# Transposing the last four pairs of h0 by DMA in a graph layer on one NeuronCore

## The reference

```
h0  = relu(layernorm(x))
agg = adj @ h0                                  # the aggregate
h   = h0 @ W_sa ;  sl = h @ a_left ;  sr = h @ a_right
e   = where(adj != 0, exp(-leaky_relu(sl[:, None] + sr[None, :], 0.01)), 0)
x_a = (e @ h) / (sum(e, axis=1) + 1e-5)
x_b = agg @ W_gcnb + b_gcnb
attn_a = sigmoid([agg, h0] @ Wa.T + ba) ; attn_b the same with Wb, bb
out = x + sigmoid(attn_a * x_a + attn_b * x_b)
```

## Time and profile before

| | us |
|---|---|
| median of 3 runs | 179.05 (178.74 to 179.24) |
| profiled execution, its own time | 178.25 |
| its span | 176.4 |
| PE busy | 171.6 |
| DVE busy | 147.0 |
| ACT busy | 115.4 |
| POOL busy | 18.6 |

### The profile page before, as it was taken

How to read it: one execution, slowest core, us unless ns; L and a number is a source line. 1 busy time by engine, 2 the same in 40 slices (tenths; PEclk the granted TensorE clock), 3 DMA queues, 4 the chain that set the end, 5 groups by cost and what they waited for, 6 DMA issues and landing times.

```text
span 176.4 us, 3397 instructions
## 1 busy us (share of the span) xinstructions
PE 171.6 (97%) x1324; PEld 125.8 (71%) x1324; DVE 147.0 (83%) x309; ACT 115.4 (65%) x169; POOL 18.6 (11%) x42
## 2 busy tenths in 40 slices
PE   7999999999999999999999999999999999999992
PEld 2556776654444468888844488888888888888892
DVE  3799997648999999799999922999999999976551
ACT  3679899642899988748494640675875884863310
POOL 4745436030000200000000000000000000000000
PEclk9999999999999999999999999999999999999999
DMA  5999996999991598000001100000010010011101
GB/s 129 288 260 260 224 181 116 202 206 211 298 423 43 82 214 180 0 4 2 0 4 59 59 0 4 0 0 0 4 59 0 6 59 0 4 61 59 60 33 30
DMA packets 5520, 16.87 MB, mean 96 GB/s; under 512 B 625, under 2 KB 1409, under 8 KB 4737
## 3 DMA queue, kind: packets, MB, share of 16 engines
q0 software_dynamic: 1584, 8.39, 24.6%
q1 hardware_dynamic: 3920, 8.27, 13.2%
HBM read 22.94 MB, written 2.11 MB: 142 GB/s over the span
## 4 chain that ended last, share of the span: by engine, by line
PE 94%; DMA 3%; DVE 1%; SPq 1%; issue 0%; ACT 0%; DVEq 0%
PE ps L773 31%; PE ps L815 16%; PE ps L816 16%; PE ps L814 16%; PE ps L751 6%; PE ps L807 6%; DMA wa_sb<-in_w_wide 3%; PE ps L745 2%; SPq L234 1%; PE ps L877 0%; DVE wa_hi L507 0%; DVE logit L724 0%; DVE e_lo L526 0%; ACT logit L411 0%; DVE res L631 0%
## 5 line engine op out<-in xcount | busy, mean ns | idle before, releaser
L814 PE MATMUL ps<-mv_lo,e_hi 128*128 128x257 f16 (+2 forms) x272 | 71.0, 267 | 0.0
L816 PE MATMUL ps<-mv_hi,e_lo 128*128 128x257 f16 (+2 forms) x272 | 70.8, 266 | 0.0
L815 PE MATMUL ps<-mv_hi,e_hi 128*128 128x257 f16 (+2 forms) x272 | 70.8, 266 | 0.0
L377 ACT ACTIVATE z<-z,log_e 128x1024 f32<-128x1024 f32 x32 | 36.7, 1146 | 29.1 <-DVE z L568 29.1
L568 DVE SCALAR_TENSOR_TENSOR z<-sl_row,exs,far 128x512 f32<-128x512 f32 x64 | 45.0, 743 | 0.0
L576 DVE TENSOR_TENSOR e_lo<-z,e_hi 128x1024 f16<-128x1024 f32 x32 | 38.9, 1216 | 1.2 <-ACT e_hi L387 1.2
L773 PE MATMUL ps<-adj,nat_lo 128*128 128x512 f16 x128 | 36.8, 379 | 0.0
L773 PE MATMUL ps<-adj,nat_hi 128*128 128x512 f16 x128 | 36.7, 379 | 0.0
L387 ACT ACTIVATE e_hi<-z 128x1024 f16<-128x1024 f32 x32 | 33.3, 1041 | 0.0
L815 PEld LDWEIGHTS ps<-mv_hi,e_hi 128*128 128x128 f16 x272 | 26.5, 98 | 3.2
L814 PEld LDWEIGHTS ps<-mv_lo,e_hi 128*128 128x128 f16 x272 | 26.4, 97 | 3.3
(11 more groups left out here) (69 smaller groups left out, 164.8 us busy)
## 6 DMA issues: line engine op xcount, KB each, us to landing
adj<-in_adj_t POOLq DMA_DIRECT2D x6, 1024.0 KB, 10.4
x_sb<-in_x SPq DMA_DIRECT2D x6, 512.0 KB, 8.9
out<-res SPq DMA_DIRECT2D x7, 256.0 KB, 2.0
adj<-in_adj_t POOLq DMA_DIRECT2D x3, 512.0 KB, 7.5
x_sb<-in_x SPq DMA_DIRECT2D x3, 256.0 KB, 4.8
sl_row<-sl_line SPq DMA_DIRECT2D x1, 768.0 KB, 9.7
adj<-in_adj_t POOLq DMA_DIRECT2D x2, 256.0 KB, 5.9
wa_sb<-in_w_wide SPq DMA_DIRECT2D x1, 258.0 KB, 4.5
```

The lines of the kernel that those rows point to most:

```text
L377: act.activation(z[:, n % ZRING, :, :], z[:, n % ZRING, :, :], ACT.Exp, bias=log_e[:, 0:1], scale=SLOPE - 1.0).then_inc(exp_done, 1)
L814: pe.matmul(ps[:, bank, cols], e_hi[:, s, i1], mv_lo[:, j, cols], start=(j == 0), stop=False)
L815: pe.matmul(ps[:, bank, cols], e_hi[:, s, i1], mv_hi[:, j, cols], start=False, stop=False)
L816: return pe.matmul(ps[:, bank, cols], e_lo[:, s, i1], mv_hi[:, j, cols], start=False, stop=(j == NT - 1))
```

## The change

- Only units 0 to 4 (pairs 0 to 3) are still transposed by PE. For pairs 4 to 7, SP issues two transposing DMAs a pair, one from nat_hi into h0t_hi, one from nat_lo into h0t_lo, 128 partitions x 512 f16 each (turn_by_dma). ACT and DVE no longer copy these four pairs out of PSUM.
- The wide products of these four pairs leave the pair loop of chunk 0. They stand in the second aggregate, behind 8, 10, 13 and 16 of its 16 tiles. Their narrow_results, mv_highs and mv_lows move between the exponential steps n = 2 to 7.
- The sl row is made in two halves of 8 tiles. The first half is turned on PE behind pair 5 of chunk 0, and its store stands on SP behind the transposes of pairs 4, 5 and 6, its spread behind those of pair 7. The second store stands behind the reload of x.
- On POOL, load 5 is issued before norms(6) where it stood behind it, and loads 7 and 8 wait until all eight transposing DMAs have landed.
- h0t is laid out tile by tile. The adding of 0.5 to x (half_added) moves to steps 8, 9, 11 and 12.

```diff
-SL_PARTS = ((0, 4), (4, 16))
+SL_PARTS = ((0, 8), (8, 16))
+LATE = 4
+ONTIME = NPAIR - LATE
+NTURN = NU - LATE
-WIDE_BANKS = (6, 2)
+WIDE_BANKS = (6, 2, 6, 2, 0, 2, 0, 2)
@@ SP
+            def turn_by_dma(p):
+                ts = slice(2 * p, 2 * p + 2)
+                for have, nat, h0t in ((nat_high, nat_hi, h0t_hi), (nat_ready, nat_lo, h0t_lo)):
+                    sp.wait_ge(have, p + 1)
+                    sp.dma_start(h0t[:, ts, :, :].rearrange("p t k n -> p (t k) n"),
+                                 nat[:, ts, :].rearrange("p t d -> p (t d)"),
+                                 transpose=True).then_inc(h0t_landed[p - ONTIME], 16)
+
+            sp.wait_ge(adj_landed[piece_of(0, NT - 1)], 16)
+            turn_by_dma(4)
+            turn_by_dma(5)
+            turn_by_dma(6)
             sl_store(0)
+            turn_by_dma(7)
             sl_spread(0)
-            sl_store(1)
-            sp.wait_ge(turned, NU)
+            sp.wait_ge(adj_landed[piece_of(2, 0)], 16)
+            sp.wait_ge(turned, NTURN)
...
+            sl_store(1)
             sl_spread(1)
@@ POOL
             norms(5)
+            load_adj(5)
             norms(6)
-            load_adj(5)
             norms(7)
             norms(8)
             load_adj(6)
+            for p in range(ONTIME, NPAIR):
+                pool.wait_ge(h0t_landed[p - ONTIME], 32)
             load_adj(7)
             load_adj(8)
@@ ACT
-            for p in range(1, NPAIR):
...
+            for p in range(1, ONTIME):
+                if p + 2 < NTURN:
                     h0t_highs(p + 2)
+                h0_tiles(p + 3)
+                nat_highs(p + 2)
+                if p < ONTIME - 1:
+                    mv_highs(p)
+            h0_tiles(NU - 2)
+            nat_highs(NPAIR - 2)
+            mv_highs(ONTIME - 1)
+            h0_tiles(NU - 1)
+            nat_highs(NPAIR - 1)
+            sl_lines(0)
             agg_highs(0)
...
+                if n == 2:
+                    mv_highs(4)
+                if n == 3:
+                    mv_highs(5)
+                if n == 5:
+                    mv_highs(6)
                 if n == 6:
+                    mv_highs(7)
@@ DVE
+                if ONTIME <= n < NPAIR:
+                    dve.wait_ge(exs_ready, n + 1)
...
+                if n == 2:
+                    narrow_results(4)
+                if n == 3:
+                    mv_lows(4)
+                    narrow_results(5)
+                if n == 4:
+                    mv_lows(5)
+                if n == 5:
+                    narrow_results(6)
+                if n == 6:
+                    mv_lows(6)
+                    narrow_results(7)
                 if n == 7:
+                    mv_lows(7)
+                if n == 8:
                     agg_lows(1)
@@ PE
                 b_pair(p)
-                if p + 1 < NPAIR:
+                if p + 2 < NTURN:
                     turn(p + 2)
-                wide(p + 1)
-            b_products(1, 0, 4)
-            pe.wait_ge(h0t_ready, NU)
-            sl_lines(1)
-            b_products(1, 4, 16)
-            b_products(2, 0, 16)
+                if p + 1 < NTURN:
+                    wide(p + 1)
+                if p == 5:
+                    pe.wait_ge(mv_ready, 6)
+                    sl_lines(0)
+            b_products(1, 0, 8)
+            pe.wait_ge(h0t_ready, NTURN)
+            wide(5)
+            b_products(1, 8, 10)
+            wide(6)
+            b_products(1, 10, 13)
+            wide(7)
+            b_products(1, 13, 16)
+            wide(8)
+            b_products(2, 0, 4)
+            sl_lines(1)
+            b_products(2, 4, 16)
```

More of the change, by code:

```diff
@@ L53 @@
 NU = len(UNITS)
-SL_PARTS = ((0, 4), (4, 16))
-SL_UNIT = 4
-SL_BANKS = (2, 0)
+SL_PARTS = ((0, 8), (8, 16))
+SL_BANKS = (6, 0)
 SL_COLS = slice(BANK - P, BANK)
 X_PARTS = ((0, 1), (1, 2), (2, 4), (4, 6), (6, 8), (8, 12), (12, 16))
-WIDE_BANKS = (6, 2)
+LATE = 4
+ONTIME = NPAIR - LATE
+NTURN = NU - LATE
+WIDE_BANKS = (6, 2, 6, 2, 0, 2, 0, 2)
 B_BANKS = (4, 6, 4, 4)
@@ L119, in build @@
         e_lo = sb("e_lo", [P, 2 * ESLOT, CW], F16)
-        h0t_hi = e_hi[:, 16:24, :].rearrange("p (k s) n -> p k (s n)", k=KT)
-        h0t_lo = e_lo[:, 16:24, :].rearrange("p (k s) n -> p k (s n)", k=KT)
+        h0t_hi = e_hi[:, 16:24, :].rearrange("p s (a k n) -> p (s a) k n", k=KT, n=P)
+        h0t_lo = e_lo[:, 16:24, :].rearrange("p s (a k n) -> p (s a) k n", k=KT, n=P)
         zeros = e_hi[:, 0, :]
@@ L136, in build @@
         part_b = sb("part_b", [P, 2, D], F32)
-        sl_turn = [part_b[0:hi - lo, h, 0:P] for h, (lo, hi) in enumerate(SL_PARTS)]
+        sl_turn = [c_sb[0:hi - lo, C_WT + h * P:C_WT + (h + 1) * P] for h, (lo, hi) in enumerate(SL_PARTS)]
         gated_b = sb("gated_b", [P, 2, 2, D], F32)
@@ L172, in build @@
         h0t_ready = sem("h0t_ready")
+        h0t_landed = [sem(f"h0t_landed{p}") for p in range(ONTIME, NPAIR)]
         wide_product = sem("wide_product")
@@ L219, in turn_bank, with h0t_tiles @@
             n = (UNITS[u][1] - UNITS[u][0]) * P
-            return ps[:, u % 2, 0:KT * n].rearrange("p (k n) -> p k n", k=KT)
-        def h0t_cols(tile, u):
-            return tile[:, :, UNITS[u][0] * P:UNITS[u][1] * P]
+            return ps[:, u % 2, 0:KT * n].rearrange("p (t k n) -> p t k n", k=KT, n=P)
+        def h0t_tiles(tile, u):
+            return tile[:, UNITS[u][0]:UNITS[u][1], :, :]
         def wide_bank(t):
-            return WIDE_BANKS[t // 2 % 2] + t % 2
+            return WIDE_BANKS[t // 2] + t % 2
         block = ctx.enter_context(nc.Block())
@@ L344, in h0t_highs @@
                 act.wait_ge(turned, u + 1)
-                act.activation(h0t_cols(h0t_hi, u), turn_bank(u), ACT.Copy).then_inc(h0t_high, 1)
+                act.activation(h0t_tiles(h0t_hi, u), turn_bank(u), ACT.Copy).then_inc(h0t_high, 1)
             def nat_highs(p):
@@ L353, in mv_highs @@
                 act.wait_ge(exs_ready, p + 1)
-                if p == SL_UNIT - 1:
-                    sl_lines(0)
                 act.activation(scale_a[:, 2 * p:2 * p + 2], exs[:, 2 * p:2 * p + 2, SR], ACT.Exp, bias=log_s[:, 0:1],
@@ L442, in _ @@
                     act_high(n - 1)
-                if n in (2, 3, 4):
-                    half_added(n - 2)
+                if n == 2:
[4 more added lines that the diff above has]
+                    mv_highs(6)
                 if n == 6:
+                    mv_highs(7)
+                    act.activation(factor_l[:, :], exs[:, :, SL], ACT.Exp, scale=SLOPE).then_inc(factors_done, 1)
+                if n == 7:
                     agg_highs(1)
-                    half_added(3)
+                if n == 8:
+                    sl_lines(1)
+                if n in (8, 9, 11, 12):
+                    half_added((8, 9, 11, 12).index(n))
                 if n == 10:
@@ L525, in h0t_lows @@
                 dve.wait_ge(h0t_high, u + 1)
-                dve.tensor_tensor(h0t_cols(h0t_lo, u), turn_bank(u), h0t_cols(h0t_hi, u), ALU.subtract).then_inc(h0t_ready, 1)
+                dve.tensor_tensor(h0t_tiles(h0t_lo, u), turn_bank(u), h0t_tiles(h0t_hi, u), ALU.subtract).then_inc(h0t_ready, 1)
             def nat_lows(p):
@@ L562, in dve_z @@
                 if j == 0:
-                    dve.wait_ge(sl_ready[min(c, 1)], 16)
+                    dve.wait_ge(sl_ready[c // 2], 16)
                 if n >= ZRING:
@@ L651, in _ @@
             mv_lows(0)
-            for p in range(1, NPAIR):
-                if p + 1 < NPAIR:
-                    nat_lows(p + 1)
+            for p in range(1, ONTIME - 1):
+                nat_lows(p + 1)
                 if p > 1:
                     mv_lows(p - 1)
-                if p + 4 < NU:
-                    moments(p + 4)
+                moments(p + 4)
                 narrow_results(p)
-                if p + 1 < NPAIR:
-                    h0t_lows(p + 2)
-            mv_lows(NPAIR - 1)
+                h0t_lows(p + 2)
+            moments(NU - 2)
+            nat_lows(ONTIME)
+            mv_lows(ONTIME - 2)
+            moments(NU - 1)
+            narrow_results(ONTIME - 1)
+            for p in range(ONTIME + 1, NPAIR):
+                nat_lows(p)
+            mv_lows(ONTIME - 1)
             agg_lows(0)
@@ L743, in turn @@
                     for k in range(KT):
-                        cols = slice((t - UNITS[u][0]) * P, (t - UNITS[u][0] + 1) * P)
-                        ins = pe.transpose(turn_bank(u)[:, k, cols], x_sb[:, t, k * P:(k + 1) * P], ident[:, :])
+                        ins = pe.transpose(turn_bank(u)[:, t - UNITS[u][0], k, :], x_sb[:, t, k * P:(k + 1) * P], ident[:, :])
                 ins.then_inc(turned, 1)
@@ L750, in wide_part @@
                     for k in range(KT):
-                        ins = pe.matmul(ps[:, wide_bank(t), cols], h0t[a][:, k, t * P:(t + 1) * P], wa2[b][:, k, cols],
+                        ins = pe.matmul(ps[:, wide_bank(t), cols], h0t[a][:, t, k, :], wa2[b][:, k, cols],
```

(9 more changed lines are left out.)

## The result

The changed kernel takes 190.3 us (median of 6, 188.8 to 193.9) against 179.15 for the kernel before: a ratio of 1.062 (95% interval 1.056 to 1.067). It is slower by 11 us, in the predicted direction, inside the stated range of 177 to 192 and near its upper end; the forecast of 185.0 was 5.3 us too low. The loss is thus nearly twice the forecast one, 11 us where 6 were forecast.

What follows compares the result with a forecast made beforehand. PE work plus PE's waits was taken to bound the kernel: 178.25 less 1.76 for turns, plus 6.7 wait at wide(7) and 1.0 clock, gives 184.2 profiled, 185.0 median; range 177.0 to 192.0 us.

Steps and rivals of the forecast that it cites:

- The bound: Time is PE work plus PE's waits; four turns removed from PE are worth 1.76 us, any new wait lost in full.
- PE's due times: PE's queue laid out: chunk 0 ends at 29.3, wide(7) is due at 43.2, a_pair(0) at 62.3.
- ACT and DVE ahead of it: ACT reaches the sl copy at 27.7 and ends it at 27.9; last pair of chunk 0 just served, cost nothing.
- Load 5: Adjacency load needed at 29.3, taken to land at 28.5 to 30.5; up to 1.2 us, only delaying wide(7)'s due time.
- The wait at wide(7): wide(7) on PE needs mv_lows(4) behind z(0) on DVE, so begins no earlier than R + 9.9: 49.9, 6.7 us late.
- R, the landing of the sl row: First sl row: store issued at 28.0, spread at 32.4, landing 7.6 later, R = 40.0; own range 36.5 to 45.5.
- The clock: PE's idle time may bring back the low clock level; price between nothing and 2.4 us, taken as 1.0.
- The sum: 178.25 - 1.76 + 6.7 + 1.0 = 184.2 us profiled; 185.0 as a median, 0.8 above.
- The row in time (1): sl row lands by 33.3, wide(7) doesn't wait and the 1.76 us are kept: 177.3 us median, chance 0.22.
- Rival 3: Transposes slow, 3.5 us each, everything on SP's queue waits behind; wide(7) 21 us late: 198 us, chance 0.11.
- the sixth would land at 35.8: Transposes one after another at 2.3 us each: eighth lands at 40.4, store's wait some 8 us, R 43 or 45.
- all of h: a_pair(0) on PE needs it by 62.3 plus the delay; ready about R + 25, taken as covered.

Runs made afterwards that it cites:

- the run that tests it: Kernel before with 12 of the 16 turn blocks of units 5 to 8 left out: 177.8 against 178.8 us, ratio 0.9933.
- the run on ACT's queue: Changed kernel with the first store and spread of the sl row issued by ACT, transposes left on SP: 184.8 us, ratio 1.029.
- reordering run: Changed kernel with late pairs 4 and 5 ahead of the first z, pairs 6 and 7 at steps 2 to 4: 186.7 us, ratio 1.043.
- the run with the extra matmuls: Changed kernel with 44 extra 512-column matmuls, results never read, on PE in front of wide(7): 188.7 us, ratio 1.054.
- the two executions of 184.9 and 200.9 us: Changed kernel, late pairs first, sl row on ACT's queue: 184.9 with second sl copy at step 5, load 7 after pair 6; 200.9 with load 7 right behind load 6.

## Why the prediction came out as it did

- **The bound** (PE's work plus its waits): right. 16 blocks fewer on PE are worth their time (1.2 of 1.3 us in the run that tests it), and the long wait at wide(7) was lost in full.
- **PE's due times**: right. wide(7) was due at 43.2; PE got there at 43.6 and 43.0 in the runs.
- **ACT and DVE ahead of it**: right, within 1 us. The sl copy was ready at 28.9 in the changed kernel and 27.3 in the run on ACT's queue, where I had 27.9.
- **Load 5**: it cost nothing. Load 6, for which I had no term, was 2.2 us late in the profiled execution of the change and in no other profile.
- **The wait at wide(7)** and its form R + 9.9: right, 10.07 in each of three runs. The reordering run shows it for a wait of order: with the same DMAs it is gone.
- **R, the landing of the sl row**: the term that was mis-sized. I had 40.0; it was 43.3 in the run with the extra matmuls and 43.8 in the reordering run, which have the change's SP queue. The failing step is "if a transposing one costs as much, SP is free and the store goes at 28.0": it went at 35.3 and 35.8 in these two. A transposing DMA holds its queue for 1.27 us even in quiet, and up to 5 beside loads. In the run with extra matmuls the store was thus 7.3 us late, and luck hid over half of this error: the spread could go 3.1 us after the store, where I had 4.4, and landed in 4.9 (3.5 to 5.3 over the runs), where I had 7.6. So R was off by only 3.3.
- **The clock**: 1.0 taken, 2.7 measured, a little over my bound of 2.4. The granted clock was 0.50 after 50 us, with PE idle, and 1.00 in the same stretch of the run with extra matmuls. The Trainium skill's rule (TensorE: Matmul & The Clock Gate, Part 1: The HAM clock gate), that the clock follows how busy the array has lately been, agrees with both.
- **The sum**, made again with the sizes of the run with extra matmuls: 178.25 - 1.76 + 9.8 + 2.7 + 0.4 (PE is there at 43.6 in place of 43.2) = 189.4, and 0.8 for the median: 190.2. Measured 190.3.
- **The rivals.** The row in time (1) would have needed R of 33.3; the best run had 38.2. Rival 3 came about in part. Its mechanism, that everything on SP's queue waits behind the transposes, is what made the row late; its size, 3.5 us each, was too high: the six held SP for 2.2 us each on average (21.9 to 35.3, run with extra matmuls), just under the 2.3 from which I had it leave my range. The prediction also named, and did not take, the case "the sixth would land at 35.8", with R of 43 or 45. The transposed tiles themselves were in time in the change; the two executions of 184.9 and 200.9 us above show how near they are to being late.

What the prediction did not see at all, and what did no harm to its number, is that ACT's second sl copy, at step 8, was the next late thing, 5.4 us at a_pair(0). It listed "all of h" as that product's need and not the copy, though the code names it. It was hidden behind wide(7)'s wait.

Left open is what sets the 1.27 us of an issue, and why it grows to 5 and 10 in the middle of the six. No run held the size of a packet, the number of loads or the number of transposes already in flight apart from the rest.

## What to carry to other kernels

Before a chain of tiny DMAs is put on a queue behind other DMAs, price the issue of those and not only their landing; the queue that issues is a resource like an engine. When work is postponed into a stage that begins with a wait, put it ahead of that wait, or everything that depends on it inherits the wait: here order alone was worth nearly 11 us. And after one wait is removed, list every semaphore of the next consumer, since the next late one is already there.

## What the runs showed of the hardware

- A transposing DMA of 128 x 512 f16 from SBUF to SBUF holds SP's queue for 1.27 us in quiet and for 1.3 to 4.9 (5.8 and 10.3 in two long executions) behind others of its kind and beside adjacency loads; it lands in 2.4 us alone, in 12.7 beside two loads of 1024 KB that began with it, and in 26.0 at worst.
- At the same places it lands about as fast as a plain copy of as many bytes: medians of 7.7 and 6.0 us against 5.9 and 7.2. It differs in what it costs the issuing queue, where the plain copies took 0.5 to 1.0 us each.
- It moves its 128 KB in some 544 packets, about 240 bytes each on average.
- A 4 KB store behind six plain copies, with two more behind it and loads in flight, kept SP waiting until 7.5 us after its issue (28.18 to 35.68).
- After a wait of 10.5 us PE worked at 0.50 of its clock for another 5.6 us, which cost 2.7 us; extra matmuls in the wait took this away.
